# Spline stages: the second calibration and choice by halves of the tokens, and the knots below counted by one sum on VectorE

## The reference

```
x = x + 0.5 * _L1_ffn_ref(_layernorm(x), ...)      # fourth and sixth sublayer

def _calibrate(scores, knots, temperature):        # 8 knots
    idx_float = sigmoid(scores / (temperature[0] + 1e-06)) * (K - 1)
    idx_low = clip(idx_float.astype(int32), 0, K - 2)
    t = idx_float - idx_low
    return knots[idx_low] + t * (knots[idx_low + 1] - knots[idx_low])

cluster_gates = _calibrate(xf @ cluster_sigs.T)    # 8 clusters
cluster_idx = argmax(cluster_gates)
tile_gates = _calibrate(xf @ sigs.T)               # 64 tiles, 8 for each cluster
local_idx = argmax(tile_gates of the chosen cluster)
tile_idx = cluster_idx * 8 + local_idx
comp = tanh(gelu(xf @ compress_w1 + b1) @ compress_w2 + b2)
mag = relu(comp @ spline_w1[tile_idx] + spline_b1[tile_idx]) @ spline_w2[tile_idx] + spline_b2[tile_idx]
y = layernorm(xf + mag * directions[tile_idx] * output_scale) * gamma + beta
```

## Time and profile before

| | us |
|---|---|
| median of 3 runs | 2871.42 (2870.7 to 2874.26) |
| profiled execution | 2877.28 |
| its span | 2875.5 |
| VectorE busy in the span | 2047.4 (71%) |
| TensorE busy (matmuls) | 2357.5 (82%) |
| ScalarE busy | 1841.8 (64%) |
| GpSimd busy | 928.1 (32%) |

### The profile page before, as it was taken

The page is one execution under the profiler, slowest core; times in us unless marked ns, Lnnn a source line. Parts: engine busy times, 40 slices in busy tenths (PEclk is TensorE's granted clock), DMA queues, the critical chain, the costliest instruction groups (busy, mean ns, idle before and its releaser), DMA issues. The chain is left out here.

```text
span 2875.5 us, 44593 instructions
## 1 busy us (share of the span) xinstructions
PE 2357.5 (82%) x13383; PEld 1207.3 (42%) x13383; DVE 2047.4 (71%) x5859; ACT 1841.8 (64%) x4699; POOL 928.1 (32%) x1259
## 2 busy tenths in 40 slices
PE   3667765838888878599999999997958888888888
PEld 3345544512222236344444444444424444444453
DVE  4526544769999957666666666665778999998855
ACT  2123313327777774477777777776559999999955
POOL 2442255354344333500000000003734444444427
PEclk9778677659999997799999999999979999999979
DMA  6320322022323300000000000000011111111001
GB/s 189 96 76 8 100 77 80 1 43 58 72 49 69 63 12 1 31 1 1 1 1 1 1 1 1 1 1 1 1 35 30 30 30 30 31 30 31 1 1 30
DMA packets 227661, 94.65 MB, mean 33 GB/s; under 512 B 175778, under 2 KB 215522, under 8 KB 227426
## 3 DMA queue, kind: packets, MB, share of 16 engines
q1 hardware_dynamic: 218592, 82.61, 12.1%
q0 software_dynamic: 3584, 7.58, 1.0%
q10 hardware_dynamic: 5250, 1.62, 0.3%
HBM read 30.66 MB, written 19.17 MB: 17 GB/s over the span
## 5 line engine op out<-in xcount | busy, mean ns | idle before, releaser
L2562 ACT ACTIVATE s_pT<-s_ps_t 128x512 f32<-128x512 f32 x1024 | 625.8, 639 | 142.3 <-PE s_ps_t L2150 124.0
L2310 DVE TENSOR_REDUCE s_neg_max<-s_ps_a 128x1 f32<-128x512 f32 x1024 | 666.3, 682 | 63.7 <-PE s_ps_a L2116 53.8
L2553 ACT ACTIVATE s_first<-s_ps_a,s_neg_max 128x512 f32<-128x512 f32 x512 | 391.0, 764 | 24.7 <-DVE s_neg_max L2310 23.2
L2162 PE MATMUL s_ps_t<-ident,s_first 128*128 128x128 f32 x2048 | 317.5, 285 | 82.1 <-ACT s_pT L2562 69.5
L2894 DVE CUSTOM_DVE_ANT_0 s_e<-s_ps_a,w_alibi 128x128 f32<-128x128 f32 (+3 forms) x512 | 231.2, 489 | 187.0 <-PE s_ps_a L2739 186.8
L2481 POOL TENSOR_SCALAR s_first<-s_first,s_rec 128x512 f32<-128x512 f32 x128 | 232.1, 1813 | 368.1 <-DVE s_rec L2316 362.1
L3010 ACT ACTIVATE s_e<-s_e,s_neg_max 128x128 f32<-128x128 f32 (+3 forms) x512 | 283.0, 556 | 42.4 <-DVE s_neg_max L2894 40.9
L2116 PE MATMUL s_ps_a<-s_lanesT 64*128 64x512 bf16 x1024 | 275.4, 401 | 38.8 <-DMA s_lanesT<-n_lanes 22.1
L2162 PEld LDWEIGHTS s_ps_t<-ident,s_first 128*128 128x128 f32 x2048 | 221.3, 142 | 181.8 <-ACT s_pT L2562 140.4
L2180 PE MATMUL s_ps_o<-s_pT,n_v_pad 128*32 128x512 f32 x2048 | 278.9, 618 | 12.2 <-ACT s_oT L2568 12.2
L3020 ACT ACTIVATE s_pT<-s_ps_t 128x512 f32<-128x512 f32 (+3 forms) x512 | 195.5, 434 | 123.1 <-PE s_ps_t L2751 122.8
(11 more groups left out here) (423 smaller groups left out, 4121.4 us busy)
## 6 DMA issues: line engine op xcount, KB each, us to landing
s_y_rows<-s_zeros SPq DMA_DIRECT2D x4, 2048.0 KB, 10.7
s_parts<-s_y_rows SPq DMA_DIRECT2D x32, 256.0 KB, 4.0
s_token_rows<-s_rows SPq DMA_DIRECT2D x4, 1088.0 KB, 5.7
s_Wi<-L_ffn_experts_inter SPq DMA_DIRECT2D x2, 1792.0 KB
x<-L_attn_x SPq DMA_DIRECT2D x4, 512.0 KB, 8.1
out<-x SPq DMA_DIRECT2D x8, 256.0 KB, 2.3
s_lanesT<-n_lanes SPq DMA_TRANSPOSE x64, 4.6
s_shiftedT<-n_lanes SPq DMA_TRANSPOSE x64, 2.4
```

Source lines behind the costliest of these rows:

```text
L2162: last = pe.transpose(st[n % NK][:, t * P:(t + 1) * P], first[:, p % NF, 2 * t + a, i * P:(i + 1) * P], G.ident[:])
L2310: dve.tensor_reduce(neg_max[:, column(n):column(n) + 1], sa[n % NA][:], AX.X, ALU.max, negate=True).then_inc(s.max_ready, 1)
L2553: act.activation(first[:, g % NF, n % PU, :], sa[n % NA][:], ACT.Exp, bias=neg_max[:, n:n + 1], accum_out=sum1[:, n % (NR * PU):n % (NR * ...
L2562: act.activation(pT[:, n % NP, :], st[n % NK][:], ACT.Exp).then_inc(s.probs_ready, 1)
```

## The change

The second calibration and choice run by halves: sixteen tiles are calibrated, chosen and written to `chosen`, and then the other sixteen. `calibrate` takes a slice `at` and a number of tiles; the part in front (scaling, the request for the exponential, the first values of `val` and `high`) has become `begin_calibration` and still runs once for all tiles. The first calibration still runs over all tiles at once. In both calibrations the five additions on GpSimd and the semaphores `over_ready` and `idx_ready` are gone; one `tensor_reduce` on VectorE sums the six tensors of `over`, between the comparisons and the predicated copies. On TensorE the ten stirs in front of both halves have become eight in front of each half, each released by its own `nearly_chosen`.

```diff
@@ -1575,7 +1575,7 @@
         sb = lambda n, shape, dt=F32: ctx.enter_context(nc.sbuf_tensor(f"{tag}_{n}", shape, dt))
         pb = lambda n, shape: ctx.enter_context(nc.psum_tensor(f"{tag}_ps_{n}", shape, F32))
         s = semaphores(nc, "v_chain p_chain var_ready rstd_ready minus_ready xn_ready x_shifted xnT_psum xnT_ready route_psum "
-                           "route_ready hidden_psum gelu_ready comp_psum tanh_ready to_exp exp_ready over_ready idx_ready "
+                           "route_ready hidden_psum gelu_ready comp_psum tanh_ready to_exp exp_ready "
                            "chosen_here chosenT_psum chosenT_ready rows_psum rows_ready directions_psum y_made "
                            "z_ready z_weighed z_taken nearly_chosen")
         N = Norm(nc, ctx, G, s, tag, [], own_xb=False, whole=B)
@@ -1606,41 +1606,42 @@
             @block.vector
             def _(dve):
                 do = Chain(dve, s.v_chain)
-                knot = lambda k: G.knots[:, k:k + 1].unsqueeze(2).to_broadcast(SH)
-
-                def calibrate(turn, scores):
+                def begin_calibration(turn, scores):
                     dve.tensor_scalar(sc[:], scores, G.inv_temp[:, 0:1], None, ALU.mult).then_inc(s.to_exp, 1)
-                    do.free(dve.tensor_copy(val[:], knot(0)))
-                    do.free(dve.tensor_copy(high[:], knot(1)))
+                    do.free(dve.tensor_copy(val[:], G.knots[:, 0:1].unsqueeze(2).to_broadcast(SH)))
+                    do.free(dve.tensor_copy(high[:], G.knots[:, 1:2].unsqueeze(2).to_broadcast(SH)))
                     dve.wait_ge(s.exp_ready, turn)
-                    do(dve.tensor_scalar(sc[:], sc[:], 1.0, None, ALU.add))
-                    do(dve.reciprocal(sc[:], sc[:]))
-                    do(dve.tensor_scalar(sc[:], sc[:], float(KINDS - 1), None, ALU.mult))
-                    if turn > 1:
-                        dve.wait_ge(s.idx_ready, turn - 1)
+
+                def calibrate(at, n, warn):
+                    knot = lambda k: G.knots[:, k:k + 1].unsqueeze(2).to_broadcast([P, n, KINDS])
+                    do(dve.tensor_scalar(sc[:, at], sc[:, at], 1.0, None, ALU.add))
+                    do(dve.reciprocal(sc[:, at], sc[:, at]))
+                    do(dve.tensor_scalar(sc[:, at], sc[:, at], float(KINDS - 1), None, ALU.mult))
                     for k in range(1, KINDS - 1):
-                        dve.tensor_scalar(over[:, k - 1], sc[:], float(k), None, ALU.is_ge).then_inc(s.over_ready, 1)
-                    dve.wait_ge(s.over_ready, (KINDS - 2) * turn)
+                        do.free(dve.tensor_scalar(over[:, k - 1, at], sc[:, at], float(k), None, ALU.is_ge))
+                    dve.wait_ge(s.v_chain, do.n)
+
+                    do.free(dve.tensor_reduce(idx[:, at], over[:, :, at].rearrange("p k t e -> p t e k"), AX.X, ALU.add))
                     for k in range(1, KINDS - 1):
                         for to, of in ((val, knot(k)), (high, knot(k + 1))):
 
                             dve.wait_ge(s.v_chain, do.n - 1 if k > 1 else do.n)
-                            do.free(dve.copy_predicated(to[:], over[:, k - 1].bitcast(I32), of))
+                            do.free(dve.copy_predicated(to[:, at], over[:, k - 1, at].bitcast(I32), of))
                     dve.wait_ge(s.v_chain, do.n)
-                    if turn > 1:
+                    if warn:
                         dve.engine_nop().then_inc(s.nearly_chosen, 1)
-                    do.free(dve.tensor_tensor(high[:], high[:], val[:], ALU.subtract))
-                    dve.wait_ge(s.idx_ready, turn)
-                    do(dve.tensor_tensor(sc[:], sc[:], idx[:], ALU.subtract))
-                    do(dve.tensor_tensor(sc[:], sc[:], high[:], ALU.mult))
-                    do(dve.tensor_tensor(val[:], val[:], sc[:], ALU.add))
-
-                def first_of_greatest(out):
-                    do(dve.tensor_reduce(mx[:], val[:], AX.X, ALU.max))
-                    do(dve.tensor_tensor(val[:], val[:], mx[:].unsqueeze(2).to_broadcast(SH), ALU.is_equal))
-                    do(dve.tensor_tensor(val[:], val[:], G.desc[:].unsqueeze(1).to_broadcast(SH), ALU.mult))
-                    do(dve.tensor_reduce(mx[:], val[:], AX.X, ALU.max))
-                    do(dve.tensor_tensor(out, val[:], mx[:].unsqueeze(2).to_broadcast(SH), ALU.is_equal))
+                    do.free(dve.tensor_tensor(high[:, at], high[:, at], val[:, at], ALU.subtract))
+                    do(dve.tensor_tensor(sc[:, at], sc[:, at], idx[:, at], ALU.subtract))
+                    do(dve.tensor_tensor(sc[:, at], sc[:, at], high[:, at], ALU.mult))
+                    do(dve.tensor_tensor(val[:, at], val[:, at], sc[:, at], ALU.add))
+
+                def first_of_greatest(out, at, n):
+                    wide = [P, n, KINDS]
+                    do(dve.tensor_reduce(mx[:, at], val[:, at], AX.X, ALU.max))
+                    do(dve.tensor_tensor(val[:, at], val[:, at], mx[:, at].unsqueeze(2).to_broadcast(wide), ALU.is_equal))
+                    do(dve.tensor_tensor(val[:, at], val[:, at], G.desc[:].unsqueeze(1).to_broadcast(wide), ALU.mult))
+                    do(dve.tensor_reduce(mx[:, at], val[:, at], AX.X, ALU.max))
+                    do(dve.tensor_tensor(out[:, at], val[:, at], mx[:, at].unsqueeze(2).to_broadcast(wide), ALU.is_equal))
 
                 def take_cluster():
 
@@ -1690,13 +1691,19 @@
                     N.tile_statistics(dve, do, G.x, b)
                     N.aggregate(dve, do, b)
                 dve.wait_ge(s.route_ready, B)
-                calibrate(1, route[:, :, 0:KINDS])
-                first_of_greatest(cl[:])
+                whole = slice(0, NT)
+                begin_calibration(1, route[:, :, 0:KINDS])
+                calibrate(whole, NT, False)
+                first_of_greatest(cl, whole, NT)
                 take_cluster()
-                calibrate(2, sc[:])
-                first_of_greatest(lo[:])
-                for b in range(0, B, 2):
-                    choose(b)
+                begin_calibration(2, sc[:])
+
+                for h in range(HALVES):
+                    at = slice(h * HT, (h + 1) * HT)
+                    calibrate(at, HT, True)
+                    first_of_greatest(lo, at, HT)
+                    for b in range(h * HB, (h + 1) * HB, 2):
+                        choose(b)
                 for b in range(B + 2):
                     if b < B:
                         if b % HB == 0:
@@ -1718,15 +1725,6 @@
                     do(pool.tensor_tensor(minus[:, at], N.mv[:, at, 0], N.rstd[:, at], ALU.mult))
                     pool.tensor_scalar(minus[:, at], minus[:, at], -1.0, None, ALU.mult).then_inc(s.minus_ready, 1)
 
-                def knots_below(turn):
-                    for k in range(1, KINDS - 2):
-                        pool.wait_ge(s.over_ready, (KINDS - 2) * turn + k + 1)
-                        op = pool.tensor_tensor(idx[:], over[:, 0] if k == 1 else idx[:], over[:, k], ALU.add)
-                        if k < KINDS - 3:
-                            do(op)
-                        else:
-                            op.then_inc(s.idx_ready, 1)
-
                 def shift_x(b):
                     pool.wait_ge(s.xn_ready, TB * (b + 1))
                     pool.tensor_tensor(G.x[:, tiles(b)], G.x[:, tiles(b)],
@@ -1742,8 +1740,6 @@
                         deviations(b, 0)
                     if b >= 2:
                         shift_x(b - 2)
-                knots_below(0)
-                knots_below(1)
                 pool.wait_ge(s.x_shifted, B)
                 for b in range(B + 1):
                     if b < B:
@@ -1896,10 +1892,10 @@
                         compress_again(b - 1)
 
                 pe.wait_ge(s.tanh_ready, 2)
-                pe.wait_ge(s.nearly_chosen, 1)
-                stir(pe, G, comp_ps[:], 10)
                 for h in range(HALVES):
                     first = h * HB
+                    pe.wait_ge(s.nearly_chosen, h + 1)
+                    stir(pe, G, comp_ps[:], 8)
                     turn_chosen(first)
                     stir(pe, G, comp_ps[:], 1)
                     for b in range(first + 1, first + HB):
```

## The result

The first comparison gave 2858.64 us for the changed kernel (median of 18 runs, 2843.45 to 2870.64) against 2870.95 us for the kernel before (18 runs on the same chip, 2854.76 to 2879.68). The ratio is 0.9954, 95% interval 0.9936 to 0.9971: 12.3 us faster, and by the interval 8 to 18. The forecast was 2865.4, 6.0 us faster, with a range down to 2862.6. The scatter is wider than the three runs shown of before let one see: 25 us from the lowest to the highest.

The account below looks back on a forecast made before the run. Bound: VectorE's path in both spline stages, with 6.67 us standing still before `magnitudes(0)`. Gains of 2.5 us (first stage) and 4.1 (second), less 0.6, make 6.0 off the median of 2871.42: 2865.4 us, range 2862.6 to 2870.4.

Parts of the forecast that it names:

- The signs that the prediction named for being wrong: Half's sum over 1.7 us, first-half turns at the 1.2 GHz level, or VectorE waiting over 1 us for batch 3's directions.
- First calibration at zero: First calibration: VectorE about 0.7 us earlier, hidden by ScalarE's gelu chain and table load, costed at zero.
- The sum's price: VectorE's reduction over six tensors: 1.03 ns a number over a fixed 0.15 us, 1.74 us for 6 x 256.
- the first rival: Strided sum on VectorE at half speed, 0.8 us more a half; total gain 4.9 us, 2866.5 us; 12%.
- TensorE's path: From T0, the second calibration's start: first turn at T0+12.3, `magnitudes(0)` at T0+20.7, 0.5 us later than VectorE's path.
- The 0.2 us for the clock: First half on TensorE: fewer stirs leave some turns and rows at the low clock, cutting 3.0 us to 2.8 a stage.
- The second half: Eight new stirs cost TensorE 1.7 us; `result(3)` loses 0.3 us in the first stage, starting about 12.4 after `magnitudes(0)`.
- The 1.3 us of gain: Second spline stage: `result(3)` starts about 12.4 us after `magnitudes(0)` instead of 13.79, as TensorE's standing still nearly closes.
- I put the difference on the median: Whole kernel: the 6.0 us gained inside the spline stages, taken off the median of 2871.42, gives 2865.4 us.
- theory L: The change gains only what lies inside the two spline stages, some 6 us; the rest is chance of the clock elsewhere.
- theory P: Later stages fall in a fixed way better against the clock's steps once the spline stages are shorter.
- The slower rival: Clock does not rise in the first half: `magnitudes(0)` at T0+27, 3.2 us later a stage, 2877.8 us; 7%.

Follow-up runs that it names:

- before_again: The kernel before, unchanged, timed again against itself: ratio 0.9989 (0.9971 to 1.0007).
- before_steady_2: Second timing of the kernel before with eight more stirs in front of the first loop in the capacity and linear expert stages: mean 2866.1 us.
- both kernels held out of the low start: Kernel before and changed kernel, each with eight more stirs before the capacity and linear expert stages' first loops: means 2867.8 and 2859.3 us, repeated 2866.1 and 2858.2.
- sum_only: Kernel before with only the sum moved to VectorE; second calibration whole, ten stirs once: ratio 1.0014 (0.9991 to 1.0038).
- sum_steady: sum_only with eight more stirs in front of the first loop in the capacity and linear expert stages: mean 2861.7 us.
- halves_only: Changed kernel with the knot counting given back to GpSimd, a half at a time: ratio 0.9979 (0.9958 to 1.0000), mean 2859.2 us.
- the padded kernels: Both kernels with extra expert-stage stirs, plus unused VectorE reciprocals ending each spline stage: changed kernel 2865.5 us (2.8 us a stage), kernel before 2863.6 us (1.79).
- the missing second stirs: Changed kernel with extra expert-stage stirs, without the eight stirs in front of the second half: mean 2864.7 us, 5.4 us slower than with them.
- after_3: The changed kernel, unchanged, timed again against the kernel before: mean 2857.3 us, ratio 0.9966 (0.9943 to 0.9988).

## Why the prediction was wrong in size

The forecast step that failed is the fifth below. The signs that the prediction named for being wrong hardly appeared: the sum over a half took 1.45 us and not over 1.7, VectorE waited 0.21 and 0.56 us for the directions of batch 3 and not over 1, and of the first half's turns only four in the second stage ran at the low level (1.02 us where the later ones took 0.60). All these signs look inside the spline stages, and the missing 6 us lie outside.

- **First calibration at zero: held.** It became 0.3 us longer, not 0.7 shorter, and ScalarE hid that too.
- **The sum's price: mis-sized.** I took 1.03 ns a number from reductions over consecutive numbers and put the copy of 32 numbers above the rule on lines. 6 x 128 numbers took 1.45 us, not 0.94, and 6 x 256 took 2.76, not 1.74: 1.7 ns a number. The Trainium skill, "SBUF — State Buffer", section Specifications (TRN2), which speaks of a penalty for a new 16-byte line at each access, fits this; the short copy could not show it over its fixed 0.15 us. The three additions over consecutive numbers, 1.2 us for the same sum, agree. VectorE's second half therefore ended at T0+21.3 and not at T0+20.2, and became the later path. This is the first rival in a milder form: 0.5 us more a half where it had 0.8. It takes 0.4 us from the saving of a stage, 2.4 in place of 2.8.
- **TensorE's path: held.** First turn at T0+12.25 (12.3 forecast); `magnitudes(0)` at T0+21.3 (20.9), set by VectorE. The 0.2 us for the clock did not show, since VectorE was later.
- **The second half: held in its times, with luck in the gain.** `result(3)` 12.19 and 12.54 us behind `magnitudes(0)` (12.4 forecast), and the 13.79 of the second stage of before did not come back in the changed kernel's own three profiles. It was not there in before_again either (12.12), but again in before_steady_2 (13.72): in two of the six profiles built on the kernel before. The 1.3 us of gain exist only against such an execution; against before_again the changed kernel's second stage is 0.4 us later at this place.
- **"I put the difference on the median": this step failed.** The two stages gained 5.2 to 6.4 us by their barriers, close to the 6.0. But I took everything outside them as fixed, a term put at nothing without a reason, and it is not fixed. The last stage takes about 87 us, or 101 us when it starts low. Both profiles of the kernel before have the long one; all three of the changed kernel have the short one. In the first comparison 17 of 18 runs of the kernel before lay above 2864, on the chip of before_steady_2 16 of 35. Three runs between 2870.7 and 2874.3 looked like a kernel that repeats itself, and I gave the swing of stages at either level of the clock no place in the sum or the range. With both kernels held out of the low start, the distance is 8.2 us (8.5 and 7.9), not 12; their last stages take 86.6 to 90.8 us.
- **What fills the rest, as far as it is known.** If a run at 0.912 or less over its whole length is one with the low start, the kernel before has it in 40% of its runs (70 of 175) and the changed one in 21% (9 of 42). With 14 us for each that makes 2.6 us in the mean, an estimate from these counts and the two lengths. Added to the 8.2 it gives 10.8, the mean of the three distances without stirs (13.3, 7.5 and 11.5). And some 2 us of the 8.2 lie outside the spline stages. One untouched stage stands out there, the second narrow attention: 679.6 to 682.1 us in the six profiles of kernels built on the one before, 677.4 to 679.6 in the fourteen built on the changed one, 1.9 us apart in the mean (give or take 0.5). It isn't the halves, since sum_only and sum_steady have 679.1 and 679.0, nor the two semaphores fewer, since halves_only has them back and takes 678.5. So neither theory holds whole: theory L leaves out these 2 us and the share of low starts, and of a fixed gain in later stages, theory P, only the narrow attention shows anything.
- **What stays open.** Why the kernel before falls into the low start more often, and by how much: the share differs from set to set (10 of 35 to 19 of 35), and the changed kernel has only 42 runs. Why the narrow attention differs. The near nothing of the padded kernels, which in the profiles stands in the wide attention and the last stage. And the 5.4 us of the missing second stirs.
- **The slower rival**, that the clock would not rise, did not come: the granted clock over the 9 us behind the first half's stirs was 0.99 in the first stage and 0.95 in the second, and the latest `magnitudes(0)` in any profile with halves was T0+21.92.

## What to carry to other kernels

When a wait at the end of a producer's chain and a chain that only starts with its last product stand one behind the other, cut the producer in two: VectorE's 6.7 us of standing still paid for the second half, and in the stages' lengths the halves alone gave nearly all of the gain. Before a forecast of a few microseconds in a kernel of several stages, look for stages that can run at either level of TensorE's clock; their swing (14 us here) belongs in the range, even when the change does not touch them. Price a reduction by its stride, not by its count alone.

## What the runs showed that I had not expected

A loop of turns, stirs and thin products can stay at the 1.2 GHz level for 30 us though TensorE is hardly ever idle in it (10.00 of 10.00 us busy at 0.50 in two of the three stretches), and the same loop rises to the 2.4 GHz level within 5 us in another execution. It isn't decided by the stage's first rows: before_again and after_3 begin alike, with turns of 0.63 us and then 1.06. Eight more stirs in front cut the deviation between runs from 5 to 12 us to 2 to 4. GpSimd's five additions lengthened six comparisons from 1.30 us to 2.38, though VectorE waited for none of them. And the same kernel's mean differed by 8 us between sets of runs (2863.9 to 2871.7), of which 5.6 us on one and the same chip (2866.1 and 2871.7). Effects below that can only be compared within a set.
